# Scans that write over their decays in PSUM: reads all on VectorE, pair sums on GpSimd, one product for ranks and rows

## The reference, cut to what matters

```python
xs = jax.nn.silu(xc.transpose(0, 2, 1))             # 256 channels
delta = jax.nn.softplus(xs @ wd1.T @ wd2.T + wd2_b) # through a rank of 64
A = -jnp.exp(A_log)                                 # 256 x 16
Bm = xs @ wb.T                                      # 16 numbers a token
Cm = xs @ wc.T                                      # 16 numbers a token
def step(h, inp):
    d_l, b_l, c_l, x_l = inp
    h = jnp.exp(d_l[:, :, None] * A) * h + (d_l * x_l)[:, :, None] * b_l[:, None, :]
    return (h, jnp.einsum('ben,bn->be', h, c_l))    # y sums over the 16 states
_, ys = lax.scan(step, h0, ...)
```

## Time and profile before

| what | us |
|---|---|
| median of 3 runs (lowest, highest) | 2452.4 (2448.72, 2458.42) |
| the profiled execution | 2451.05 |
| its span | 2449.3 |
| mean granted clock of TensorE | 0.944 of full |

### The profile page before, as it was taken

One profiled execution on the slowest core, in us unless ns is written; L12 is line 12 of the kernel. 1 busy time (PEld: TensorE's weight loads), 2 busy tenths in 40 slices (PEclk: granted clock), 3 DMA queues, 4 the chain that ended last, 5 costly groups with the idle time before them and its releaser, 6 DMA issues. The chain is left out here.

```text
span 2449.3 us, 33072 instructions
## 1 busy us (share of the span) xinstructions
PE 2167.2 (88%) x11302; PEld 1547.8 (63%) x11302; DVE 1669.1 (68%) x3253; ACT 1234.2 (50%) x2710; POOL 1018.8 (42%) x815
## 2 busy tenths in 40 slices
PE   7888777899799999999997595767999999999998
PEld 3565556688698988898897484322554545545554
DVE  6667555677666676667765694599687877869921
ACT  6231222499544454554453352556566565655543
POOL 5000000121122233233322463689687777868722
PEclk9799899899899999999998696898999999999999
DMA  9500000000000000000000234333333324334311
GB/s 352 165 1 0 1 1 1 1 1 1 20 1 1 1 11 11 1 11 11 9 4 11 68 104 161 97 112 97 108 104 96 113 91 117 110 94 121 95 35 35
DMA packets 77151, 145.25 MB, mean 59 GB/s; under 512 B 9432, under 2 KB 31080, under 8 KB 75944
## 3 DMA queue, kind: packets, MB, share of 16 engines
q1 hardware_dynamic: 72600, 133.67, 17.7%
q0 software_dynamic: 4384, 9.46, 1.2%
HBM read 130.91 MB, written 31.65 MB: 66 GB/s over the span
## 5 line engine op out<-in xcount | busy, mean ns | idle before, releaser
L224 ACT ACTIVATE TMP<-ps,W 128x512 f32<-128x512 f32 (+2 forms) x784 | 457.1, 614 | 391.5 <-PE ps L209 225.6
L209 PE MATMUL ps<-TMP,W 128*128 128x512 f32 (+5 forms) x1232 | 612.8, 604 | 42.3 <-ACT TMP L227 9.4
L209 PE MATMUL ps<-TMP 128*128 128x65 f32 (+5 forms) x4354 | 514.9, 286 | 6.6 <-DVE W L229 4.4
L209 PEld LDWEIGHTS ps<-TMP 128*128 128x128 f32 (+3 forms) x4354 | 474.6, 192 | 52.5 <-issue 17.5
L233 POOL TENSOR_TENSOR TMP<-TMP 128x512 f32<-128x512 f32 (+1 forms) x176 | 227.9, 1298 | 588.0 <-ACT TMP L224 435.6
L209 PEld LDWEIGHTS ps<-TMP,W 128*128 128x128 f32 (+3 forms) x1232 | 218.3, 188 | 250.7 <-issue 152.8
L233 POOL TENSOR_TENSOR TMP<-TMP,W 128x512 f32<-128x512 f32 x256 | 356.9, 1418 | 30.4 <-DVE TMP L2874 29.3
L209 PE MATMUL ps<-TMPr,Wr 128*128 128x512 f32 x768 | 320.0, 524 | 5.6 <-ACT TMP L224 5.6
L209 PE MATMUL ps<-TMPr 128*128 128x512 f32 (+4 forms) x1032 | 266.3, 404 | 34.0 <-DVE TMPr L229 23.1
L209 PEld LDWEIGHTS ps<-TMPr 128*128 128x128 f32 (+2 forms) x1032 | 192.9, 197 | 84.3 <-issue 23.2
L209 PEld LDWEIGHTS ps<-TMPr,Wr 128*128 128x128 f32 x768 | 145.0, 190 | 140.9 <-issue 116.0
(11 more groups left out here) (239 smaller groups left out, 3114.3 us busy)
## 6 DMA issues: line engine op xcount, KB each, us to landing
W<-rows SPq DMA_DIRECT2D x224, 256.0 KB, 3.6
sorted<-pad SPq DMA_DIRECT2D x8, 2304.0 KB
XK<-gates SPq DMA_DIRECT2D x64, 256.0 KB, 3.5
TMP<-rows SPq DMA_DIRECT2D x32, 256.0 KB, 3.3
TMP<-sorted SPq DMA_DIRECT2D x72, 72.0 KB, 2.0
W<-wp SPq DMA_DIRECT2D x1, 4124.0 KB, 14.8
XK<-results SPq DMA_DIRECT2D x16, 256.0 KB, 3.8
W<-wp SPq DMA_DIRECT2D x1, 3072.0 KB, 27.1
```

The source lines that it names most:

```text
L209: return nc.tensor.matmul(out, lhsT, rhs, start=start, stop=stop, **k)
L224: return nc.scalar.activation(out, x, f, bias=bias, scale=scale)
```

## The change

- The scan writes its states over its decays: output and first input are both `Ab[x]` in PSUM. The four buffers `Hb` are gone.
- All 32 reads of a chunk are on DVE, right behind their scan, and take the state from PSUM. `Cb` has eight buffers instead of six. The next decay of the same half waits for the read instead of for the scan, and the value carried to the next chunk is taken from `Ab[x]`, again after the read.
- A new POOL step "pair" adds the products of states 2p and 2p + 1, and "tail" adds one pair instead of one state: 16 tails in a chunk instead of 32.
- "bc" and its copy are gone: the weights `wd1`, `wb` and `wc` lie beside each other in `wnT`, and "rank" makes 96 rows at once (64 of the rank, 32 of B and C), in one of two buffers `Nw`. The product for delta reads all 96 rows against weights with 32 rows of zeros; "rows_out" stores rows 64 to 95.
- `first_unit` is 59, and many steps beside the scan stand one slot later.

The diff, cut to its core:

```diff
-        Bb, Cr, Ub, Hb, Cb = (more(n) for n in (4, 4, 6, 4, 6))
-        narrow = ar(512)
-        d1, Bw = narrow[0:64, :], [narrow[64 + 32 * j:96 + 32 * j, :] for j in range(2)]
+        Bb, Cr, Ub, Cb = (more(n) for n in (4, 4, 6, 8))
+        Nw = [ar(512) for _ in range(2)]
-        by_pool = lambda g: g % 16 % 3 == 1
-        first_unit = 32 + 26
+        first_unit = 32 + 27
...
             if 0 <= g < GN:
-                plan.append(("scan", (g, s)))
-                if s:
-                    plan.append(("read", (g, 0)))
+                plan += [("scan", (g, s)), ("read", (g, s))]
             plan += gated(u - 2) + joined(u - 3)
-            if 0 <= g - 2 < GN:
-                plan.append(("tail", (g - 2, s)))
+            if q >= 4 and q % 4 < 2 and q // 4 - 1 < GN // 2:
+                plan.append(("pair", (q // 4 - 1, q % 4)))
+            k = (q - 6) // 2
+            if 0 <= k < GN and s == 0:
+                plan.append(("tail", divmod(k, 2)))
...
-                    mm(Yp[x], w("ident"), Cb[(2 * g + x) % 6], False, n == 15).then_inc(*y_pe(a))
+                    mm(Yp[x], w("ident"), Cb[(4 * p + x) % 8], False, n == 7).then_inc(*y_pe(a))
...
                     if g:
-                        e.wait_ge(*h_dve.at((g - 1, x)))
+                        e.wait_ge(*hc_dve.at((g - 1, x)))
+                        if (g - 1) // 16 % 2 == 0:
+                            e.wait_ge(*c_act.at((g - 1, x)))
                     act(Ab[x], ch(sets[i % 2][2], x), ACT.Exp, ...).then_inc(*a_act(a))
...
-                    nc.vector.tensor_tensor_scan(Hb[q % 4], Ab[x], Ub[q % 6], first, ALU.mult, ALU.add)...
-                elif step == "read" and not by_pool(a[0]):
+                    nc.vector.tensor_tensor_scan(Ab[x], Ab[x], Ub[q % 6], first, ALU.mult, ALU.add)...
+                elif step == "read":
...
-                    if g >= 3:
-                        e.wait_ge(*y_pe.at((g - 3, x)))
-                    tt(Cb[q % 6], Cr[g % 4], Hb[q % 4], ALU.mult).then_inc(*hc_dve(a))
+                    if g >= 4:
+                        e.wait_ge(*(hp_pool if g % 2 else y_pe).at(((g - 4) // 2, x)))
+                    tt(Cb[q % 8], Cr[g % 4], Ab[x], ALU.mult).then_inc(*hc_dve(a))
...
-                    gtt(Cb[q % 6], Cr[g % 4], Hb[q % 4], ALU.mult).then_inc(*hc_pool(a))
+                elif step == "pair":
+                    p, x = a
+                    k = (4 * p + x) % 8
+                    e.wait_ge(*hc_dve.at((2 * p + 1, x)))
+                    gtt(Cb[k], Cb[k], Cb[k + 2], ALU.add).then_inc(*hp_pool(a))
```

More of the change, by code:

```diff
@@ L2365, in hand_over @@
             n = norm(7, i)
-            put(q + 5, ("out", i))
-            put(q + 6, ("result", i))
-            put(q + 7, n[0])
-            put(q + 8, n[1])
-            put(q + 9, n[2])
-            put(q + 10, n[3])
-            put(q + 12, n[4])
-            put(q + 13, n[5])
-            put(q + 14, n[6])
-            put(q + 15, n[7], ("split", i))
-            put(q + 16, ("shift", i))
-            put(q + 18, ("probs", i))
-            put(q + 19, ("route", (i, 0)))
-            put(q + 20, ("route", (i, 1)))
-            put(q + 22, ("route", (i, 2)))
-            put(q + 24, ("row", i))
-            put(q + 25, ("row_out", i))
-            put(q + 27, ("table", i))
-            put(q + 28, *[("fetch", 8 * i + k) for k in range(3)])
+            put(q + 6, ("out", i))
+            put(q + 7, ("result", i))
+            put(q + 8, n[0])
+            put(q + 9, n[1])
+            put(q + 10, n[2])
+            put(q + 11, n[3])
+            put(q + 13, n[4])
+            put(q + 14, n[5])
+            put(q + 15, n[6])
+            put(q + 16, n[7], ("split", i))
+            put(q + 17, ("shift", i))
+            put(q + 19, ("probs", i))
+            put(q + 20, ("route", (i, 0)))
+            put(q + 21, ("route", (i, 1)))
+            put(q + 23, ("route", (i, 2)))
+            put(q + 25, ("row", i))
+            put(q + 26, ("row_out", i))
+            put(q + 28, ("table", i))
+            put(q + 29, *[("fetch", 8 * i + k) for k in range(3)])
         def norm_ahead(i, q):
@@ L2407, in scan_moe_stage @@
         plan += both("shut") + norm(6, 1)[:3]
-        plan += [("rank", 0), ("bc", 0), ("rank_out", 0), ("bc_out", 0)] + both("delta")
+        plan += [("rank", 0), ("rank_out", 0)] + both("delta")
         plan += [("softplus", (0, 0)), ("softplus", (0, 1)), ("exp", 0), ("log", 0), ("dx", 0), ("rows_out", 0)]
@@ L2470, in scan_moe_stage @@
                 plan.append(("decay", (g + 1, s)))
-            if s and 0 <= g < GN:
-                plan.append(("read", (g, 1)))
             plan += down(u - 1)
@@ L2483, in scan_moe_stage @@
         I = range(NCH)
-        rk_pe, rk_act, bc_pe, ex_act, ln_act, dl_dve, dx_pool, out_pe, res_dve = (
-            Sig(sem("s7_" + n), I) for n in ("rank_pe", "rank", "bc_pe", "delta_exp", "delta_log", "delta", "dx", "out_pe", "out"))
+        rk_pe, rk_act, ex_act, ln_act, dl_dve, dx_pool, out_pe, res_dve = (
+            Sig(sem("s7_" + n), I) for n in ("rank_pe", "rank", "delta_exp", "delta_log", "delta", "dx", "out_pe", "out"))
         de_pe, mx_act, ab_act = (Sig(sem("s7_delta_" + n), of(plan, "delta")) for n in ("pe", "max", "abs"))
@@ L2489, in scan_moe_stage @@
         GE = [(g, e) for g in G for e in range(2)]
-        raw_act = Sig(sem("s7_b_rows"), I)
-        a_act, u_pool, h_dve, y_pe = (Sig(sem("s7_" + n), GE) for n in ("decay", "input", "state", "y_sum"))
-        hc_dve, hc_pool = (Sig(sem("s7_read_" + n), [(g, e) for g, e in GE if by_pool(g) == p]) for n, p in (("dve", False), ("pool", True)))
-        read = lambda g, x: (hc_pool if by_pool(g) else hc_dve).at((g, x))
+        PE2 = [(p, e) for p in range(GN // 2) for e in range(2)]
+        a_act, u_pool, h_dve, hc_dve = (Sig(sem("s7_" + n), GE) for n in ("decay", "input", "state", "read"))
+        hp_pool, y_pe = Sig(sem("s7_pair_sum"), PE2), Sig(sem("s7_y_sum"), PE2)
         c_act = Sig(sem("s7_carried"), [(g, e) for g, e in GE if g // 16 % 2 == 0])
@@ L2520, in scan_moe_stage @@
         for s, a in plan:
-            if s in ("open", "conv", "rank", "bc", "delta", "centre", "back", "back2", "logits", "out", "row"):
+            if s in ("open", "conv", "rank", "delta", "centre", "back", "back2", "logits", "out", "row"):
                 takers.append((s, a))
-        first_bank = {("conv", (0, 0)): 7, ("conv", (0, 1)): 5, ("rank", 0): 6, ("bc", 0): 4, ("delta", (0, 0)): 7, ("delta", (0, 1)): 5,
+        first_bank = {("conv", (0, 0)): 7, ("conv", (0, 1)): 5, ("rank", 0): 6, ("delta", (0, 0)): 7, ("delta", (0, 1)): 5,
                       }
@@ L2532, in scan_moe_stage @@
             holder[bank_no(*t)] = t
-        let_go = {"open": gt_dve, "conv": ev_act, "rank": rk_act, "bc": raw_act, "delta": ab_act, "back": n_xa, "back2": n_xk,
+        let_go = {"open": gt_dve, "conv": ev_act, "rank": rk_act, "delta": ab_act, "back": n_xa, "back2": n_xk,
                   "logits": n_lgs, "out": res_dve, "row": rw_act}
@@ L2886, in dve @@
                     z = ch(dl, x)
[L2887 removed]
+                    e.wait_ge(*y_pe.at((8 * i + 7, x)))
                     e.wait_ge(*a_act.at((16 * i + 15, 1)))
```

101 lines of the change are left out of this document (38 added, 63 removed), and 2 rows, old and new, of the table GROUPS.

## The result

The changed kernel takes 2427.89 us (median of 4 runs, 2423.88 to 2432.48) against 2451.27 us before (median of 4, 2448.72 to 2458.42). The ratio is 0.9897, its 95% interval 0.9877 to 0.9917: 1.0% faster, where the prediction said 2.9% (2380 us, range 2355 to 2426). The sign was right, the size was not, and the time lies just above the range. The profiled execution took 2432.48 us, its span 2430.6 us.

The account below looks back on a forecast made before the run. PE was taken to bound the chunks with scans and units side by side; terms of -72.5 us, mostly -64.5 from five middle chunks, took 2451.05 to 2378.5, with 1.35 for the runs' median 2380 us, range 2355 to 2426.

Parts of the forecast that it names:

- The bound: Chunks with scans and units side by side: PE is the later engine, busy 102.4 of 105.4 us.
- The prologue: Stage start to first scan: second copy and its product ahead of delta go, -1 us (between -3 and 0).
- Scan, read, head, pair and join: Operation times on DVE and POOL: scan 1.21 us, read 0.68, head 1.28, pair 1.27, join about 1294 ns.
- rival 3: DVE's scan within one PSUM bank is slow, 2.4 us a scan: 2580 us, slower than before; chance 0.07.
- The meeting at gated: Where PE and DVE meet every four slots: PE idle 5.6 us a chunk instead of 3.0, period 92.5.
- Rival 4: TensorE's granted clock falls to 0.95 in phase B through stalls, 26 us longer: 2406 us; chance 0.04.
- rival 1: DVE becomes the later engine, each burst costs 9 us of PE per chunk: period 99, 2421 us; chance 0.17.
- Chunk 7: Last chunk of the scan: DVE bounds it, 80 us instead of 88.5, -8.5 us (between -11 and -3).
- Chunks 0 and 1: First two chunks: phase A +2 us for tighter order, slots 58 to 63 -2.5 for three tails less; -0.5.
- the end: After the last scan, units only: 59 slots instead of 58, +2 us.

Follow-up runs that it names:

- the merged product alone: The kernel before with only "rank" and "bc" made one product of 96 rows; 2486.97 us against 2499.28, ratio 0.9942.
- the wider spacing: The changed kernel, nothing left out, with opens, gates, routing steps, row and ScalarE's next norm part in later slots; 2389.57 us, ratio 0.9739 to the kernel before.
- the first spacing: The changed kernel with "open", gates and second routing part one slot later, routing's exponential its own step; 2448.19 us against 2499.28 before, ratio 0.9788.

## Why the prediction was wrong

**What held.** The bound (PE, in five chunks) is shown by the merged product alone. The prologue came at -1.2 for -1. Scan, read, head, pair and join came within 40 ns of their values, so rival 3 (a slow scan in PSUM, 2580 us) is out at 1.224 us. PE's work of 86.9 us a chunk is that of the wider spacing, to the tenth, but this is in part luck: "bc" took 3.4 us with it and not 1.7, and the clock was 0.98 and not full, and the two errors nearly cancel. DVE came at 81.6 for 79, POOL at 76.0 for 79.

**The step that failed** is "The meeting at gated": the charge of 2.6 us more idle time of PE per chunk. It was 7.1 (10.1 in place of 3.0). The prediction had the right parts before it: small operations of 1.15 us behind POOL, a burst of 11 us that no longer fits, a slack that falls from 3.1 to 1.8 us. It then charged this as a lag at one meeting, in DVE's queue only. Two things were left out.
- The burst is not of a fixed length. Each small operation waits for the operation of POOL that it meets, and with the pair sums it meets more of them: 8.1 us a chunk in place of 6.1, and 4.9 with the pair sums out. Beside these 2 us, the change puts two more reads and one more gate into the stretch ahead of the late "gated", which went from 12.5 to 15.8 us in the chunk shown. I had "no two-input reads left on DVE" and took it to mean that DVE and POOL no longer meet; the two-input operations of routing are left.
- DVE's lag reaches PE by a second way. ACT's queue holds, behind the operation that waits for "shift", two table loads of 1.28 us, a logarithm, a decay, a "hid" and the copy of a bank. I had followed ACT to "hid" alone, although the chain of before goes through ACT's table load. This stall of up to 4.4 us is the longer of the two; moving steps by one slot removed it and 4 us a chunk. The series from "gated" to the copy took 10.1 us before as well: it was not lengthened, PE comes to it earlier, and only in part by the fewer tails.

**The clock.** Rival 4 put it at 0.95 and gave it 4 in 100, with the words that the stalls are about 1 to 3 us each. They are 3.6 to 3.9 and 4.2 to 4.4 us, and it is 0.95. In numbers: PE's work is 89.4 us a chunk in place of 86.9, 2.5 us. The clock itself costs more than that, about 4.5 us by an estimate from the merged product's 98.7 us at full clock less 13.8 for the tails; the unforeseen 1.7 us of "bc" hide most of the difference. The Trainium skill (TensorE: Matmul & The Clock Gate, on HAM oscillation) says that PE kernels which wait again and again can fall back to half clock; the trace agrees, since the products behind both stalls took 2.08 and 2.07 us for 1.13. Before the change, with waits of at most 1.8 us, the clock was full. The length of the wait alone does not decide it: with routing out a product behind 2.59 us took 2.07, and with the reads halved one behind 3.60 us took 1.12. What else decides it was not found.

So rival 1 and rival 4 came together: 4.5 us of idle time too little (10.1 against 5.6) and 2.5 of PE's work make the 7.0 us by which a chunk misses 92.5, and five chunks 35 of the 46.5 us. They had been given 0.17 and 0.04 as if one shut out the other, but the lower clock was seen behind the stalls of the first. That rival 1's time of 2421 us is near the 2427.89 measured is luck in part: it had 9 us of stalls and no loss of clock.

**The other terms.** Chunk 7: its 88.5 us were read from a window that began at 2240, while the chunk's first scan is at 2244.9 and it lasts 83.6; 4.9 us of it were counted twice. The rest, 87.7 us in place of 80, is with DVE busy 83.0 of 89.8 us and the clock at 0.94. I had DVE's work fall by 1.3 us there; from first scan to last it rose from 75.2 to 80.9. Chunks 0 and 1 took 2.8 us more than charged, the end 5 less; neither was followed up.

**What is open.** Why other products got shorter with the merged product; what beside the length of a wait brings the lower clock; and which of the moves of the first spacing removed the stall at the copy.

## What to carry to other kernels

When work is taken off the engine that sets the end, look for the bursts on the next engine, not at its load: 6.3 us taken from DVE's burst brought 7.7 us a chunk, 8.0 us taken evenly brought 2.3. Read the short pieces of the chain of waits too, since they name the engines that are just behind, and follow a late instruction through every in-order queue behind it, table loads included; price a stall of some microseconds on TensorE with the clock that it can cost behind it. And when a change shortens the period, space the steps of the pipeline anew: here that was worth 33 us, more than the change itself (30 on that chip).
